# Two-layer graph network: the tables made from src alone, the pick mask and the cleared rows move from VectorE to GpSimd

## The reference

```python
def _L0_gnn_ref(x, edge_src, edge_dst, edge_w, W, b):
    h = x @ W + b
    msgs = edge_w[:, None] * h[edge_src]
    agg = jax.ops.segment_sum(msgs, edge_dst, num_segments=N_NODES)
    deg = jax.ops.segment_sum(edge_w, edge_dst, num_segments=N_NODES)
    return jax.nn.relu(agg / (deg[:, None] + 1e-06))

def _L1_gnn_ref(node_features, edge_features, W_msg, b_msg, W_upd, b_upd, eps, src, tgt):
    msg_in = jnp.concatenate([node_features[src], edge_features], axis=-1)
    messages = jax.nn.gelu(msg_in @ W_msg + b_msg)
    agg = jax.ops.segment_sum(messages, tgt, num_segments=node_features.shape[0])
    h = (1.0 + eps) * node_features + agg
    return jax.nn.gelu(h @ W_upd + b_upd)

h = jnp.maximum(_layernorm(x, axis=-1), 0.0)
x = x + _L0_gnn_ref(h, src, dst, edge_weight, L0_gnn_W, L0_gnn_b)
h = jnp.maximum(_layernorm(x, axis=-1), 0.0)
x = x + _L1_gnn_ref(h, edge_attr_64, L1_gnn_W_msg, ..., src, dst)
```

## Time and profile before

| | us |
|---|---|
| median of 3 runs | 2657.76 |
| lowest, highest of them | 2650.05, 2657.79 |
| the profiled execution's own time | 2652.2 |
| its span, first to last instruction | 2650.4 |
| of that: up to 84 us, prologue | 84 |
| 84 to 1060 us, about, layer one | 976 |
| from 1150 us, layer two's loop | 1500 |

### The profile page before, as it was taken

The page is one execution under the profiler, slowest core; times in us unless marked ns, Lnnn a source line. Parts: engine busy times, 40 slices in busy tenths (PEclk is TensorE's granted clock), DMA queues, the critical chain, the costliest instruction groups (busy, mean ns, idle before and its releaser), DMA issues.

```text
span 2650.4 us, 72326 instructions
## 1 busy us (share of the span) xinstructions
PE 2471.7 (93%) x22389; PEld 2315.3 (87%) x22390; DVE 2091.9 (79%) x4502; ACT 1564.2 (59%) x5144; POOL 1802.8 (68%) x1879
## 2 busy tenths in 40 slices
PE   1699999988889899899999999999999999999998
PEld 1699999888888888799999999999999999999998
DVE  8888888888888888677777777777777777777775
ACT  2366655555666666456566566566566565656653
POOL 3277755577777777177777777777777777777772
PEclk9999988898999999799999999999999999999999
DMA  6111110011111111144544444444445445544452
GB/s 123 29 25 27 24 21 18 18 26 24 28 26 25 25 24 27 45 114 117 124 120 117 124 120 118 123 118 120 121 118 122 119 117 122 120 118 120 118 122 59
DMA packets 472283, 213.84 MB, mean 81 GB/s; under 512 B 264668, under 2 KB 441656, under 8 KB 472196
## 3 DMA queue, kind: packets, MB, share of 16 engines
q1 hardware_dynamic: 412548, 151.55, 21.8%
q0 software_dynamic: 59648, 61.20, 12.7%
HBM read 207.09 MB, written 5.51 MB: 80 GB/s over the span
## 4 chain that ended last, share of the span: by engine, by line
PE 57%; DVE 0%; ACT 0%; issue 0%; DVEq 0%
PE ps L926 42%; PE ps L1131 7%; PE ps L996 4%; PE ps L1120 3%; PE ps L1078 0%; PE ps L1025 0%; DVE rows L1466 0%; DVE parts L1227 0%; DVE sel L1462 0%; DVE room L1668 0%; ACT h_sb L856 0%; DVE h_sb L1699 0%; DVE h_sb L1704 0%; ACT h_sb L874 0%; DVE tick L1503 0%
## 5 line engine op out<-in xcount | busy, mean ns | idle before, releaser
L636 POOL DMA_INDIRECT rows<-p_table,idx x1176 | 1109.7, 944 | 390.2 <-issue 344.3
L926 PE MATMUL ps<-parts,pick_all 128*128 128x448 f32 x5488 | 1161.5, 368 | 2.2 <-DVE parts L1227 2.2
L926 PEld LDWEIGHTS ps<-parts,pick_all 128*128 128x128 f32 x5488 | 1018.0, 188 | 78.3 <-issue 2.6
L636 POOL DMA_INDIRECT rows<-h_table,idx x688 | 676.8, 984 | 355.7 <-issue 189.5
L936 PE MATMUL ps<-hot_c,hot_p 128*128 128x75 f32 (+4 forms) x2400 | 458.1, 294 | 53.5 <-issue 40.0
L728 ACT COPY adj<-ps 128x500 f32<-128x500 f32 (+4 forms) x880 | 353.4, 450 | 179.1 <-PE ps L936 160.4
L1462 DVE TENSOR_TENSOR sel<-ps,mask 128x896 f32<-128x896 f32 x196 | 213.9, 1092 | 300.8 <-PE ps L926 292.7
L936 PEld LDWEIGHTS ps<-hot_c,hot_p 128*128 128x128 f32 x2400 | 386.3, 203 | 69.8 <-issue 54.9
L1445 DVE TENSOR_SCALAR pick_all<-src_all,node_f 128x1792 fp32r<-128x1792 int16 x196 | 406.5, 2075 | 27.9 <-issue 25.1
L1399 DVE TENSOR_SCALAR hot_p<-iota_p,scal 128x256 fp32r<-128x256 f32 (+1 forms) x880 | 319.0, 363 | 44.5 <-PE ps L936 24.0
L1466 DVE TENSOR_REDUCE rows<-sel 128x128 f32<-128x896 f32 x196 | 342.7, 1748 | 6.7
(11 more groups left out here) (181 smaller groups left out, 2451.7 us busy)
## 6 DMA issues: line engine op xcount, KB each, us to landing
src_all<-keys SPq DMA_DIRECT2D x196, 448.0 KB
ea<-in_edge_attr_dram SPq DMA_DIRECT2D x196, 256.0 KB
rows<-p_table,idx POOLq DMA_INDIRECT x1176
rows<-h_table,idx POOLq DMA_INDIRECT x688
x_sb<-in_x_dram SPq DMA_DIRECT2D x6, 224.0 KB, 4.3
h_table<-h_sb SPq DMA_DIRECT2D x6, 224.0 KB
p_table<-h_sb SPq DMA_DIRECT2D x6, 224.0 KB
out_dram<-h_sb SPq DMA_DIRECT2D x6, 224.0 KB
```

Of the source, the lines that this page charges most:

```text
L636: nc.gpsimd.indirect_dma_start(out=rows[:, s, j, 0:D], out_offset=None, in_=table[:, :], in_offset=bass.IndirectOffsetOnAxis(ap=idx[:, s, ...
L926: last = nc.tensor.matmul(to, hot[:, k, t * P:(t + 1) * P], parts[:, part, k, :, :].rearrange("p a d -> p (a d)"), start=(k == 0 and part ...
```

## The change

GpSimd issues the first body's twelve gathers outside its loop and then runs the new function `source_numbers`. It makes `adj_tab[.., 0, ..]` and `a_tab` (semaphore `s_srcn`, for which DVE now waits), clears `wall` (`s_wall`, for which ACT now waits ahead of `copy_scal`), and makes `mask` (`s_mask`). The division by 128, a shift on DVE, becomes three arithmetic instructions on GpSimd, and the one instruction that made the mask becomes seven, one for each of its seven values. Every step of `source_numbers` but the parts of one table waits for the one before (`step`). Its scratch lies in `ea`, so SP loads the edge attributes only after the mask. DVE's `s_tables` is now signalled by a small memset of `tick`.

```diff
-            sp.wait_ge(s_tr, 2)
+            sp.wait_ge(s_mask, 1)
             for s in range(SLOTS):
                 load_ea(s, s)
...
+            def quotient(to, of, by):
+                to_whole = 1.5 * 2.0 ** 23
+                step(nc.gpsimd.tensor_scalar(to, of, 1.0 / by, -(by - 1) / (2.0 * by), ALU.mult, ALU.add))
+                step(nc.gpsimd.tensor_scalar(to, to, to_whole, None, ALU.add))
+                step(nc.gpsimd.tensor_scalar(to, to, -to_whole, None, ALU.add))
+            def source_numbers():
+                n = JA * NG
+                flat = ea[:, :, :].rearrange("p s d -> p (s d)")
+                part = flat[:, n:2 * n].rearrange("p (j g) -> p j g", j=JA)
+                second = flat[:, 0:n].rearrange("p (j g) -> p j g", j=JA)
+                pool.wait_ge(s_srct, 2)
+                pool.wait_ge(s_key, 2)
+                quotient(part, src_tab[:, 0:JA, :], P)
+                step(nc.gpsimd.tensor_scalar(second, part, float(KW) - 0.5, None, ALU.is_gt))
+                step(nc.gpsimd.tensor_tensor(tab_a[:, :, :], part, second, ALU.subtract))
+                lower = adj_tab[:, :, 0, :].rearrange("p g j -> p j g")
+                step(nc.gpsimd.tensor_scalar(tab_a[:, :, :], tab_a[:, :, :], -float(P), None, ALU.mult))
+                step(nc.gpsimd.tensor_copy(lower, src_tab[:, 0:JA, :]))
+                step(nc.gpsimd.tensor_tensor(lower, lower, tab_a[:, :, :], ALU.add))
+                step(nc.gpsimd.tensor_scalar(second, second, -float(KW), None, ALU.mult))
+                step(nc.gpsimd.tensor_tensor(part, part, second, ALU.add))
+                for z in ZONES:
+                    last = nc.gpsimd.tensor_scalar(a_tab[:, :, z.groups], part[:, :, z.groups], float(z.WT), 1.0,
+                                                   ALU.mult, ALU.add)
+                last.then_inc(s_srcn, 1)
+                pool.wait_ge(s_srcn, 1)
+                pool.wait_ge(s_dwt, 4)
+                nc.gpsimd.memset(wall, 0.0).then_inc(s_wall, 1)
+                quotient(part[:, 0:PICKS, :], src_tab[:, J0:J, :], P)
+                quotient(part[:, 0:PICKS, :], part[:, 0:PICKS, :], KA)
+                for n in range(NA):
+                    last = nc.gpsimd.tensor_scalar(mask[:, :, :, n].rearrange("p g t -> p t g"), part[:, 0:PICKS, :],
+                                                   float(n), None, ALU.is_equal)
+                last.then_inc(s_mask, 1)
...
                 if layer == 0:
+                    gathers(1, range(ZONES[0].JA, J))
+                    source_numbers()
                     for z in ZONES:
-                        with pool.Fori(z.first + 1, z.end + 1) as turn:
+                        with pool.Fori(max(z.first, 1) + 1, z.end + 1) as turn:
...
             act.wait_ge(s_tables, 1)
+            act.wait_ge(s_wall, 1)
...
-            meta(nc.vector.tensor_copy(high_i[:, :, :], src_tab[:, 0:JA, :]))
...
-            for z in ZONES:
-                meta(nc.vector.tensor_scalar(a_tab[:, :, z.groups], high_f[:, :, z.groups], float(z.WT), 1.0, ALU.mult,
-                                             ALU.add))
+            dve.wait_ge(s_srcn, 1)
...
-            nc.vector.memset(wall, 0.0).then_inc(s_tables, 1)
+            nc.vector.memset(tick[:, :], 0.0).then_inc(s_tables, 1)
...
-            meta(nc.vector.tensor_copy(keep, src_tab[:, J0:J, :]))
-            highest(keep, keep)
...
-                                    ALU.is_equal).then_inc(s_mask, 1)
```

More of the change, by code:

```diff
@@ L408, in two_layer_gnn @@
         s_mask = sem("masks_ready")
+        s_pt = sem("source_table_step")
+        s_srcn = sem("source_numbers_ready")
+        s_wall = sem("weighed_rows_cleared")
         s_sel = sem("parts_masked")
@@ L620, in _, with step @@
             nc.gpsimd.memset(sums_sb[:, :], 0.0).then_inc(s_zero, 1)
+            done = [0]
+            def step(ins):
+                done[0] += 1
+                ins.then_inc(s_pt, 1)
+                pool.wait_ge(s_pt, done[0])
+            def quotient(to, of, by):
[3 more added lines that the diff above has]
+                step(nc.gpsimd.tensor_scalar(to, to, -to_whole, None, ALU.add))
@@ L1563, in _ @@
                 build(ZONES[0], 0, s)
-            dve.wait_ge(s_srct, 2)
-            keep = high_i[:, 0:PICKS, :]
-            meta(nc.vector.tensor_copy(keep, src_tab[:, J0:J, :]))
-            highest(keep, keep)
[L1569 to L1572, removed]
-                                    ALU.is_equal).then_inc(s_mask, 1)
             dve.wait_ge(s_rowsr, 16 * sum(z.JA for z in ZONES[1:]))
```

## The result

| | before | after |
|---|---|---|
| median of 20 runs of each, us | 2657.78 | 2667.97 |
| lowest and highest | 2646.63 to 2670.18 | 2656.67 to 2677.17 |
| the profiled execution: own time, span | 2652.2, 2650.4 | 2669.83, 2668.0 |

The changed kernel takes 1.003 times as long (95% interval 1.0016 to 1.0045), about 8 us more. The time went the other way.

A forecast was written before the change was run, and what follows sets the result against it. Bound: DVE's prologue line before PE's first blocks. 3.1 us won on tables, 3.3 lost to sharing, 1.1 won on wall, 2.1 by the mask's absence: net 3.0, so 2657.76 - 3.0 = 2654.8 us; range 2645.5 to 2664.

The forecast's parts named there:

- The frame: Whole kernel: the change moves only when PE's loops begin; after that everything runs as before, earlier or later.
- GpSimd's own price: Prologue, GpSimd's a_tab chain by itself: 18.7 us, ending at 63.5; one-input instructions 1.0 each, two-input 2.0.
- my high end: GpSimd's chain with each one-input instruction doubled: 26.7 us, ending at 71.5.
- The mask: Prologue: seven GpSimd instructions of 0.6 us, done at about 78 to 80; its absence from DVE saves PE 2.1.
- Sharing: Prologue: DVE's two-input and fast instructions and GpSimd's go one at a time, cutting the gain to 3.0 us net.
- the first stretch: DVE from 49.65: six waits, 7.2 us less 1.96 DMA slack, then 0.7; leaves 3.1 of 9.05 won.
- The second stretch: DVE from 71.31 to 82.5 beside GpSimd's wall, quotients and mask: eleven waits of 0.3, 3.3 us lost.
- wall and the gap: Prologue: wall's clearing off DVE wins 1.1 us; PE's idle time between its first two batches gone, 2.1.
- The costless edits: SP's later edge loads, ACT's wait for wall and GpSimd's next gathers were to cost nothing.
- The hidden tables: Rival: GpSimd's prologue work fully hidden, the full 12.3 us gained, 2645.5 us; chance 0.20.
- The second rival: Prologue: GpSimd becomes the bound, scale-and-offset costing twice a conversion; 8.5 us slower, 2666.3; chance 0.15.
- The clock as a rival: Clock dips over 350 to 450 us could fall otherwise after a shifted start, 5 us either way; chance 0.10.

The follow-up runs named there:

- e1: Kernel before, 23 GpSimd instructions put one at a time ahead of its prologue while DVE waits, pricing each alone; 2696.09 us in one run, total not compared.
- e6: Kernel before with e5's edits, GpSimd making the tables (multiply-and-add form) before its first gathers; ratio to the kernel before 0.9965, body at 100.19 us.
- e2: Changed kernel, GpSimd's one-operation instructions given a second operation that changes nothing; one run 2669.98 us beside 2655.81 for the kernel before.
- e4: Changed kernel with the mask made by DVE again, tables and wall staying on GpSimd; body at 111.56 us, against 117.08 changed and 109.96 before.
- e5: Kernel before, wall cleared by GpSimd and DVE's mask made behind the first twenty tiles' one-hots instead of ten; ratio to the kernel before 1.0003.
- e8: Same kernel as e4, timed over 12 runs: 2656.66 us against 2658.66 for the kernel before, ratio 1.0001.

## Why the prediction was wrong

**The frame held.** PE's loops run as before, and the change is worth what the body's start moves by: 7.1 us late, inside the 4 to 12 us of the timed ratio. The test named at the prediction's end, a prologue as predicted with a cause behind 110 us, did not occur; the prologue was not as predicted.

The forecast had the body 3.0 us early and it is 7.1 late, 10.1 us apart. They split as follows.

**1. GpSimd's own price, 5.4 us: the step that failed first.** I priced seven full one-input instructions at 1.0 from the conversions. Only the first costs that. Four others take 2.66 to 2.81, one 4.08 beside DVE, the strided copy 2.99. Alone (e1) they are 2.67 and 2.22. Two inputs cost 2.25, near the 2.0 taken, and the waits between steps 0.08 instead of 0.25. The chain takes 29.3 us for 18.7 (by e1's prices some 26.6 alone, an estimate; the rest is waiting for DVE, for which I had 3), and ends at 73.50 where I had 63.5 alone and 66.5 beside DVE. Even my high end, every one-input instruction doubled, gave 71.5. DVE reached its wait at 67.45 (68.2 predicted), so the addition came at 73.61 in place of 68.2. I read the rate of one kind of instruction off another and took the spread of the unknown as a factor of two; the kernel's own forms span a factor of 2.7. I had cited the Trainium skill (GPSIMD Engine Reference, section 3) for an estimate of 2.15 us for a two-input instruction; alone it takes 2.25, so the trace agrees. Section 4.1 of that page of the Trainium skill calls one-input work on GpSimd roughly line-rate. The trace agrees for the copy and the multiply-add (1.00 and 1.01) and not for the other forms (2.67 and 3.49). What section 4.1 advises, to leave such work to VectorE, would have been the better forecast for this change, though e6 shows the tables gain on GpSimd in another place.

The 5.4 us are the share of this step in the sum. They are not what a right price would have saved: in e2 the chain takes 21.2 us and the addition comes no earlier.

**2. The mask, 4.5 us: the same mistake in a strided form.** Priced at 0.6 a slice, it takes 2.53, so it ends at 99.93, where I expected some 79. It was to save PE 2.1. Instead PE starts 0.9 later behind the tables' signal than it did (1.84 us for 0.96), and its first 80 matmuls take 21.24 us (90.17 to 111.41) for 19.71: 0.9 + 1.5 + 2.1 = 4.5. Experiment e4 puts mask and quotients at 5.5 as a whole: these 0.9 and 1.5, and 3.7 more that DVE loses between the addition and the tables' signal (14.72 for e4's 11.00), less the 0.5 by which e4's addition comes later.

**3. Sharing, 0.2 us: right in sum, wrong in its parts.** In the first stretch I had 7.2 lost in the row steps, less the slack of 1.96, and 0.7 behind them. Measured: 2.8 in three row steps (L1368, L1378, L1380), which leaves rel_tab 1.0 late, and 4.2 in the two instructions behind it (2.56 for 0.66, 4.06 for 1.79). My 5.9 against 5.2 was a lucky sum. The second stretch lost 3.5 (14.72 for 11.23), I had 3.3; e4, at 11.0, shows that all of it belongs to the quotients and the mask. That the mechanism decides was right, and e2 shows it at its worst. But e2 also shows that the forecast's numbers could hardly have come true together: beside a chain nearly as fast as I priced it (21.2 us for 18.7) the row steps lost 11.2 us, from the first of them to the copy of base_bc behind them (16.77 for 5.54), where I had 7.2.

**4. wall and the gap: right.** e5 gives back 2.3, or 3.0 from an equal start, for the 3.2 priced. That gap is hidden just as well by a later place in DVE's own order.

**5. The costless edits: right.** SP waited 25.0 us for the mask and nobody missed its loads; GpSimd's next gathers start at 113.61 after 13.69 us of idle time, so it had cover left.

**The rivals.** The hidden tables fell with the first row. The second rival, slower with GpSimd as the bound, is what happened, and its 8.5 us is close to the 7.1: L1410 is 2.3 late (3.2 given), the second stretch loses 3.5 (4.5), the one-hots and PE's gap together cost 0.9 + 1.5 (up to 4, less the gap's 2.1). Its decision point, a full one-input instruction above 1.4 us, was passed by far. I gave it 0.15, because I argued from reading and from stores (the conversion, the memset) that the rate was near the memset's. Neither row had one operation of arithmetic with a number in it. The cause that I wrote into it was the wrong way round: the scale with an offset is the cheap form, the single operation the dear one. The clock as a rival gives 11 us between executions of one kernel at its end alone, more than the 5 I allowed; it widens a comparison of single runs. That it has no part in the difference between the medians is argued from e8, whose timed ratio follows the body's start, and is not shown.

**Still open.** Why the one pair is fast and how GpSimd runs the others was not tried. That the mask's price comes of its stride rests on one dense and one strided row of e1, with outputs of different types (f32 and bf16), so the type may have a share. e2 changes the tables' form and the mask's at once, so what cheap tables with the old mask would give was not run.

## What to carry to other kernels

Before work goes to GpSimd, measure its instructions in the very form that they will have, operation pair and strides included; a conversion or a memset on the same engine tells nothing of them. Ask beside which of DVE's instructions the moved work will lie: here nearly the same chain made the addition 2.2 us late (from an equal start) beside the row steps, and 6.1 us early beside reductions and steps on one number per partition. Speeding up an engine that shares a path with the bound may only move the wait, so look at who else is in that stretch first.

## What the runs showed of the hardware

- **GpSimd's prices** for 980 f32 numbers of 128 partitions, alone: 1.01 us multiply-add, 1.00 copy, 2.25 two inputs, 2.67 one operation, 3.49 two operations of another pair, 2.22 copy with a strided output.
- **Not every GpSimd instruction keeps DVE out to its end.** DVE's L1378 ends at 55.88, with GpSimd's two-input L649 (55.84). But L1368, issued at 51.40 beside the one-operation L648, is done at 51.90, 1.1 us after L648 began and 1.6 before it ends, and the short steps after it run at their old durations. The same at L651: L1380 is done 1.1 us after its start. The Trainium skill (SBUF — State Buffer, section "Who interferes with whom") has the pair held for the whole instruction; the trace agrees for two inputs and disagrees for the one-operation form. It may be why the slow form left the row steps less disturbed than the fast one did in e2; no run takes it apart.
- **The granted clock is not PE's pace everywhere.** For 84 to 110 us the busy time by stretch reads, before and after:

```profile
84.00:110.00 26.00, 22.21 (x179) 21.72 (x179) 21.52 (x74) 9.32 (x43) 2.83 (x3) 1.00 0.02 4
```
```profile
84.00:110.00 26.00, 17.04 (x75) 16.24 (x75) 25.53 (x65) 6.53 (x28) 15.73 (x7) 0.50 0.20 41
```

1.00 is the upper level (2.4 GHz) and 0.50 the lower (1.2 GHz), yet a matmul of the first blocks takes 219 ns in both (8.78 us for 40, 11.38 for 52). From the body's start on it takes 121 ns in both (2.42 for 20). Here the durations have to be read, not the column.
